# One mask instruction for two adjacency tiles, in a two-layer graph network on one core

## The reference

```python
def gat(h, W, lw, lb, a):                 # one attention layer
    Wh = h @ W
    u, v, c = Wh @ lw[:64] @ a, Wh @ lw[64:] @ a, lb @ a
    e = leaky_relu(u + v.T + c, 0.2)      # 8192 x 8192
    att = softmax(where(adj > 0, e, -9e15), axis=1)
    return elu(att @ Wh)

# layer 0
h = relu(layernorm(x)); h0 = h; outs = [h]
for i in range(2):
    h = 0.2 * h0 + 0.8 * gat(h, W[i], lin_w[i], lin_b[i], attn[i])
    outs.append(h)
x = x + concat(outs) @ mlp_w + mlp_b
# layer 1
h = relu(layernorm(x)); a = (adj == 1)
x = x + concat(a @ h / a.sum(1), h) @ weight + bias
```

## Time and profile before

| | |
|---|---|
| time, median of 3 runs | 1733.85 us (1733.81 to 1733.99) |
| the profiled execution | 1734.81 us, span 1733.0 us, granted TensorE clock 0.971 |
| TensorE busy | 1538.9 us, 89% |
| VectorE busy | 1531.3 us, 88%, 2480 instructions |
| ScalarE busy | 1289.1 us, 74% |
| the ramps (L498) | x1024, 1149 ns each |
| on masks, off masks (L919, L929) | x512 each, 691 ns each |
| conversions (L941) | x128, 2297 ns each |

### The profile page before, as it was taken

The page is one execution under the profiler, slowest core; times in us unless marked ns, Lnnn a source line. Parts: engine busy times, 40 slices in busy tenths (PEclk is TensorE's granted clock), DMA queues, the critical chain, the costliest instruction groups (busy, mean ns, idle before and its releaser), DMA issues. The chain is left out here.

```text
span 1733.0 us, 50280 instructions
## 1 busy us (share of the span) xinstructions
PE 1538.9 (89%) x21783; PEld 1495.0 (86%) x21783; DVE 1531.3 (88%) x2480; ACT 1289.1 (74%) x1470; POOL 82.2 (5%) x118
## 2 busy tenths in 40 slices
PE   2477888888888888888799999999999999799999
PEld 2377888788888888787699999999999999799999
DVE  7899999999999999999798787869688788986665
ACT  3777898989899998989699999999999994000000
POOL 1100000101010000101100000000000000000000
PEclk9589999999999999999899999999999999999999
DMA  7988999999999999997211212122121111133231
GB/s 272 356 310 311 385 378 401 356 410 376 411 372 407 387 375 407 363 410 275 61 45 44 56 45 63 42 59 62 39 63 50 57 51 32 57 116 89 86 94 44
DMA packets 114701, 356.02 MB, mean 205 GB/s; under 512 B 8976, under 2 KB 17200, under 8 KB 114480
## 3 DMA queue, kind: packets, MB, share of 16 engines
q1 hardware_dynamic: 91040, 304.27, 46.2%
q0 software_dynamic: 8960, 29.43, 6.2%
q10 hardware_dynamic: 14480, 19.11, 3.1%
HBM read 325.45 MB, written 27.33 MB: 204 GB/s over the span
## 5 line engine op out<-in xcount | busy, mean ns | idle before, releaser
L498 ACT ACTIVATE region<-ub,bigv 128x1024 uint8<-128x1024 f32 x1024 | 1096.0, 1149 | 28.6 <-PE bank L1644 11.3
L1638 PE MATMUL bank<-wsplit,region 128*128 128x195 bf16 x8192 | 788.5, 250 | 41.3 <-DVE region L919 35.4
L1638 PEld LDWEIGHTS bank<-wsplit,region 128*128 128x128 fp8e3 x8192 | 695.2, 99 | 52.8 <-DVE region L919 35.3
L1644 PE MATMUL bank<-wsplit,region 128*128 128x130 f16 x8192 | 557.7, 221 | 52.2 <-DVE region L929 50.8
L1644 PEld LDWEIGHTS bank<-wsplit,region 128*128 128x128 fp8e3 x8192 | 500.5, 98 | 77.3 <-DVE region L929 72.5
L929 DVE SCALAR_TENSOR_TENSOR region<-region 128x512 uint32<-128x512 uint32 x512 | 343.5, 691 | 9.4 <-PE bank L1644 8.6
L919 DVE SCALAR_TENSOR_TENSOR region<-region 128x512 uint32<-128x512 uint32 x512 | 338.0, 691 | 10.1 <-ACT region L498 9.9
L941 DVE TENSOR_SCALAR region<-region 128x4096 uint8<-128x4096 int32 x128 | 294.1, 2297 | 0.9 <-DMA region<-in_adj 0.9
L1865 PE MATMUL bank<-wsplit,region 128*128 128x129 f16 x4032 | 239.6, 222 | 8.8 <-DVE region L1447 8.8
L1865 PEld LDWEIGHTS bank<-wsplit,region 128*128 128x128 fp8e3 x4032 | 237.5, 99 | 10.0 <-DVE region L1447 10.0
L1447 DVE TENSOR_SCALAR region<-region 128x512 uint32<-128x512 uint32 x256 | 100.4, 424 | 43.6 <-PE bank L1865 38.4
(11 more groups left out here) (223 smaller groups left out, 686.2 us busy)
## 6 DMA issues: line engine op xcount, KB each, us to landing
region<-in_adj SPq DMA_DIRECT2D x128, 2048.0 KB, 11.3
region<-codes_d SPq DMA_DIRECT2D x128, 256.0 KB, 2.6
codes_d<-region ACTq DMA_DIRECT2D x64, 256.0 KB, 6.5
ub<-u_d POOLq DMA_DIRECT2D x16, 512.0 KB, 7.5
hg<-h_d POOLq DMA_DIRECT2D x16, 256.0 KB, 6.3
stg<-m_d POOLq DMA_DIRECT2D x16, 256.0 KB, 4.8
region<-in_x SPq DMA_DIRECT2D x4, 512.0 KB, 6.9
h_d<-wsplit POOLq DMA_DIRECT2D x4, 512.0 KB, 4.2
```

The source lines that it names most:

```text
L498: last = nc.scalar.activation(sv[:, b, :], ub[G % 2][:, :], ACT.Relu, bias=bigv[l][:, t:t + 1], scale=BIG)
L1638: return nc.tensor.matmul(acc_on[it], columns(onb[U % NS], it, b), wsplit[:, c * TC + 2 * q + b, 0:WC], start=(c == 0 and q == 0 and b == ...
L1644: return nc.tensor.matmul(acc_off[it], columns(offb[U % NO], it, b), woff[:, c * TC + 2 * q + b, WO:WO + WF], start=(c == 0 and q == 0 and ...
```

## The change

A unit becomes one quarter of two neighbouring tiles (n even and n + 1), 4 KB per partition or 1024 words: U = LU * l + 2 * n + s, with q = 2 * (n % 2) + s. The first tile step of a pair handles quarters 0 and 1 of both tiles, the second quarters 2 and 3. So VectorE issues one on mask and one off mask of 1024 words where there were two of 512. The ring of ramps has four buffers of 4 KB, the off ring three; the bytes are the same. The mean pass keeps its buffers of 2 KB (`onm`, eight of them over the same bytes). Because a unit needs the codes of both tiles, codes and weight splits run one tile further ahead, and a codes buffer is free again only when the whole pair is masked (`pair_done`). The work of ScalarE and TensorE is the same in number and size of instructions, but its order changes: all on products of a unit (32) come before all its off products. In TensorE's wait before the small products the count rises from n + 3 to n + 4.

```diff
-LU = QC * NT
+LU = 2 * NT
-NA, NP, NS, NO = 3, 4, 8, 6
+NA, NP, NS, NO, NM = 3, 4, 4, 3, 8
...
+        def pair_done(M):
+            return 2 * (M - M % 2 + 2)
...
                 def take_codes(n):
                     act.wait_ge(tp_done, n + 1)
                     if n >= NP:
-                        act.wait_ge(off_r, 4 * (n - NP) + 4)
+                        act.wait_ge(off_r, pair_done(n - NP))
...
+                take_codes(1)
+                store_codes(1)
                 for n in range(NT):                    # ScalarE, pass 0
                     g, r = n // NCH, n % NCH
-                    ramps(0, n, 0)
-                    if g == 0 and r > 0:
-                        cast_high(0, r)
-                    ramps(0, n, 1)
-                    if n + 1 < NT:
-                        take_codes(n + 1)
+                    ramps(0, n, 0, 0)
+                    if 0 < n < NCH - 1:
+                        cast_high(0, n + 1)
+                    ramps(0, n, 0, 1)
+                    if 0 < n < NT - 2:
+                        take_codes(n + 2)
                     if r == 5 and g > 0:
                         high(NG + g - 1)
-                    ramps(0, n, 2)
-                    if n + 1 < NT:
-                        store_codes(n + 1)
-                    if g == 0 and r > 0:
-                        cast_middle(0, r)
-                    ramps(0, n, 3)
+                    ramps(0, n, 1, 0)
+                    if 0 < n < NT - 2:
+                        store_codes(n + 2)
+                    if 0 < n < NCH - 1:
+                        cast_middle(0, n + 1)
+                    ramps(0, n, 1, 1)
+                    if n == 0:
+                        take_codes(2)
+                        store_codes(2)
...
                 for n in range(1, NT):                 # ScalarE, pass 1
-                    for q in range(QC):
-                        ramps(1, n, q)
-                        if g == 0 and r > 1 and q == 0:
-                            cast_high(1, r)
-                        if g == 0 and r > 1 and q == 2:
-                            cast_middle(1, r)
+                    ramps(1, n, 0, 0)
+                    if n < NCH - 1:
+                        cast_high(1, n + 1)
+                    ramps(1, n, 0, 1)
+                    ramps(1, n, 1, 0)
+                    if n < NCH - 1:
+                        cast_middle(1, n + 1)
+                    ramps(1, n, 1, 1)
...
                 split_first(0)                         # VectorE, before pass 0
+                dve.wait_ge(p_in, 2)
+                on_mask(0, 0, 0)
+                off_mask(0, 0, 0)
                 split(0, 0)
+                split(0, 1)
                 row_args(0)
                 convert(2, 1)
                 pack_pairs(2)
                 pack(2)
+                on_mask(0, 0, 1)
+                off_mask(0, 0, 1)
+                convert(3, 0)
+                convert(3, 1)
+                pack_pairs(3)
+                pack(3)
                 for n in range(NT):                    # VectorE, pass 0
-                    ahead = n + 3 < NT
-                    dve.wait_ge(p_in, n + 1)
-                    if n + 1 < NCH:
-                        split_scaled(0, n + 1)
-                    on_mask(0, n, 0)
-                    on_mask(0, n, 1)
-                    off_mask(0, n, 0)
-                    if n + 1 < NCH:
-                        split_rest(0, n + 1)
+                    ahead = n + 4 < NT
+                    if n > 0 and n % 2 == 0:
+                        dve.wait_ge(p_in, n + 2)
+                    if n + 2 < NCH:
+                        split_scaled(0, n + 2)
+                    if n > 0:
+                        on_mask(0, n, 0)
+                    if n + 2 < NCH:
+                        split_rest(0, n + 2)
                     if ahead:
-                        convert(n + 3, 0)
-                    off_mask(0, n, 1)
+                        convert(n + 4, 0)
+                    if n > 0:
+                        off_mask(0, n, 0)
...
-                    on_mask(0, n, 2)
                     if ahead:
-                        convert(n + 3, 1)
+                        convert(n + 4, 1)
...
-                    off_mask(0, n, 2)
-                    on_mask(0, n, 3)
+                    if n > 0:
+                        on_mask(0, n, 1)
                     if ahead:
-                        pack_pairs(n + 3)
+                        pack_pairs(n + 4)
-                    off_mask(0, n, 3)
+                    if n > 0:
+                        off_mask(0, n, 1)
                     if ahead:
-                        pack(n + 3)
-                    if n + 1 < NCH:
-                        split_last(0, n + 1)
+                        pack(n + 4)
+                    if n + 2 < NCH:
+                        split_last(0, n + 2)
...
                 for n in range(NT):                    # TensorE, pass 0
-                    if n + 2 < NT:
-                        transpose_codes(n + 2)
+                    if n == 1:
+                        transpose_codes(3)
+                    if 0 < n < NT - 3:
+                        transpose_codes(n + 3)
                     unit(0, n, 0)
-                    unit(0, n, 1)
+                    if n == 0:
+                        transpose_codes(2)
                     if n == 1 or (g > 0 and r >= 5) or (g > 1 and r == 0):
-                        pe.wait_ge(p_in, min(n + 3, NT))
+                        pe.wait_ge(p_in, min(n + 4, NT))
                         claim_b7()
```

More of the change, by code:

```diff
@@ L294, in _ @@
                     M = NT + n
-                    sp.wait_ge(off_r, 4 * (M - NP) + 4)
+                    sp.wait_ge(off_r, pair_done(M - NP))
                     if n == 0:
@@ L849, in split_first, with ends, four @@
                 def split_first(l):
-                    on, off = expv[:, 0:2, 0:1].to_broadcast([P, 2, CE]), expv[:, 0:2, 1:2].to_broadcast([P, 2, CE])
-                    part = [wsplit[:, 0:2, j * CE:(j + 1) * CE] for j in range(3)]
-                    hi, lo = woff[:, 0:2, WO:WO + CE], woff[:, 0:2, WO + CE:WO + WF]
-                    full, rest, small = av[:, 0:2, :], bb[:, 0:2, :], po[:, 0:2, :]
+                    def ends(ap):
+                        return ap.rearrange("p (c k) e -> p c k e", c=2)[:, :, 0:2, :]
+                    def four(buf):
+                        return buf[:, 0:4, :].rearrange("p (c k) e -> p c k e", c=2)
+                    both = slice(0, 2 * TC)
+                    on, off = [ends(expv[:, both, i:i + 1]).to_broadcast([P, 2, 2, CE]) for i in range(2)]
+                    part = [ends(wsplit[:, both, j * CE:(j + 1) * CE]) for j in range(3)]
+                    hi, lo = ends(woff[:, both, WO:WO + CE]), ends(woff[:, both, WO + CE:WO + WF])
+                    full, rest, small = four(av), four(bb), four(po)
                     dve.wait_ge(scl, l + 1)
@@ L863, in split_first @@
                     ec.sync()
-                    sc.mark(nc.vector.tensor_tensor(full, hw[:, 0:2, :], on, ALU.mult))
-                    sc.mark(nc.vector.tensor_tensor(small, hw[:, 0:2, :], off, ALU.mult))
+                    sc.mark(nc.vector.tensor_tensor(full, ends(hw[:, both, :]), on, ALU.mult))
+                    sc.mark(nc.vector.tensor_tensor(small, ends(hw[:, both, :]), off, ALU.mult))
                     sc.sync()
@@ L1211, in _ @@
                 split(1, 0)
+                split(1, 1)
                 def old_x(e):
@@ L1329, in _ @@
                     g, r = n // NCH, n % NCH
+                    if n > 0 and n % 2 == 0:
+                        codes_in(n)
+                        codes_in(n + 1)
+                    if n + 2 < NCH:
+                        split_scaled(1, n + 2)
                     if n > 0:
-                        codes_in(n)
-                        if n + 1 < NCH:
-                            split_scaled(1, n + 1)
                         on_mask(1, n, 0)
-                        on_mask(1, n, 1)
                         off_mask(1, n, 0)
-                        off_mask(1, n, 1)
-                        if n + 1 < NCH:
-                            split_rest(1, n + 1)
+                    if n + 2 < NCH:
+                        split_rest(1, n + 2)
                     if n == 1:
@@ L1389, in _ @@
                     if n > 0:
[L1390 to L1393 removed]
+                        off_mask(1, n, 1)
+                    if n + 2 < NCH:
+                        split_last(1, n + 2)
                     if n == 1:
                         row_args(1)
[L1396 to L1397 removed]
                     if g > 0:
@@ L1674, in unit @@
                             banks_free(G, it, True)
-                        for b in range(2):
-                            last = on_matmul(l, n, q, it, b)
-                            if first and G > 0 and it == 0 and b == 0:
-                                last.then_inc(off_done, 2)
+                        for h in range(2):
```

(5 more changed lines are left out.)

178 lines of the change are left out of this document (88 added, 90 removed).

## The result

The changed kernel takes 1783.89 us (median of four runs, 1782.58 to 1784.58), the kernel before 1733.83 (1733.47 to 1733.99) beside it: a ratio of 1.0289, 95% interval 1.0277 to 1.0302. That is +50 us where +39.5 was forecast, inside the range of 1750 to 1790 and on the forecast's side. The profiled execution took 1782.58 us, its span 1780.8; what follows splits 47.8 us, from a span of 1733.0 to this one.

The account below looks back on a forecast made before the run. VectorE was taken to bound pass 0 and TensorE pass 1. The terms, -18.0 + 8.6 + 14.3 + 23.2 + 1.8 + 9.6 = +39.5 us, gave 1773 us, range 1750 to 1790.

Parts of the forecast that it names:

- Step 1: VectorE's masks in pass 0: joining 512-word masks into 1024 saves 0.30 us per tile over some 60 tiles, -18.0 us.
- Step 2: Prologue: codes one tile further ahead add conversion and weight-split time before the loop, not given back, +8.6 us.
- Step 3: Weight splits of group 0: ScalarE's codes copy waits for the last off mask, delaying casts VectorE needs, +14.3 us.
- Step 4: Each later row group: the same wait makes VectorE stall 3.4 us for ramps in seven groups, +23.2 us.
- Step 5: End of pass 0: ScalarE sets the stretch from VectorE's last mask to the last group's sums, +1.8 us.
- Step 6: Start of pass 1: casts and splits delay masks, TensorE idles 6 us, then runs at lower clock, +9.6 us.
- rival (d): Adjacency loads bind in pass 0: about 1743 us without stalls, at most a few us added with them; chance 0.06.
- Rival (a): ScalarE's lead is not needed, so slack hides the stalls in pass 0 and most later delays: 1724 us; chance 0.06.
- (b): The stall at each row group's end alone is absent because the sums fall elsewhere: 1750 us; chance 0.12.
- (c): TensorE's waits for codes reach VectorE through the off buffers, about 2.5 us more in seven groups: 1790; chance 0.12.
- (e): Neighbouring 1024-word masks overlap less than starts say; a joined pair saves 0.17 us, not 0.075: 1750; chance 0.02.

Follow-up runs that it names:

- halves: The changed kernel with each mask issued as two instructions of 512 words, same place and semaphore count: 1792.40 us, ratio 1.0333 to the kernel before.
- before_ahead: The kernel before with only the codes running one tile further ahead, masks still of 512 words: 1737.69 us, ratio 1.0024 to the kernel before.
- codes_late_g0: The changed kernel with ScalarE's codes copy moved behind the ramps at even tiles of the first row group only: 1771.28 us, ratio 1.0215.
- light_loads: The changed kernel with adjacency loads behind the first three bringing only half of each half row block (output not the reference's): 1775.75 us, ratio 1.0238.
- codes_late: The changed kernel with ScalarE's codes copy moved behind all its ramps at even tiles of pass 0: 1756.37 us, ratio 1.0126 to the kernel before.
- combo: codes_late plus, at pass 1's start, tile 1's ramps ahead of ScalarE's casts and its masks ahead of VectorE's remaining splits: 1752.16 us, ratio 1.0101.
- combo_bal: combo with each tile's second conversion moved behind its second on mask: 1751.63 us, ratio 1.0102 to the kernel before.
- late_halves: codes_late with each mask issued as two instructions of 512 words: 1763.15 us, ratio 1.0167 to the kernel before.

## Where the prediction was right and where wrong, by its steps

**Step 1** had the mechanism and nearly the size. 0.30 per tile was 0.28, VectorE's work in the 52 tiles fell by 12.7 us for 15.6, and the two trials with halves give 14.9 and 19.1 us by the medians, 17.9 and 17.8 by the spans, for the 18.0. By the estimate from the initialisation that the Trainium skill lists ("VectorE: DVE Perf Modes", "Side-by-side: where the cycles go for N=2048 bf16") it would have been 39; the trace does not agree, as the starts in the earlier trace rows had shown.

**Step 2**, 8.6 us, fits what is left of the first row of the table: 21.7, less 15.6 of waits, plus 2.2 of shorter masks, is 8.3. Its terms for the splits were not measured one by one. Its sentence that nothing is given back did not hold for the lead alone: before_ahead measured +4.0 with 5.8 at tile 8. How much of that return the changed kernel keeps was not measured.

**Step 3**, 14.3 us: the waits are 15.6, 3.1 us each at split_last as worked out, and the order of the codes copy makes 11 to 12 of them (codes_late_g0). 4.0 us at split_rest stay in that order too.

**Step 4**, 3.4 us in seven groups: 3.37 or 3.38 at five, 2.74 at the first, and 1.98 at 517.75, where VectorE had just lost 1.30 in a wait for a load (509.47) and so came later to the ramps (light_loads, which has no such wait, lost 3.36 at that place); 21.6 in all for 23.2. codes_late took 15 us more than codes_late_g0 did.

**Step 5**, +1.8 against +1.4. **Step 6**, +9.6 against +8.5, with an idle time of 5.74 us for 6.

**The sum failed in the row of 52 tiles**, 16.7 for 7.6, and the missing term is rival (d): "with them the queues have time to catch up, so at most a few us are added" ("them" are the stalls). The loads added 7.0 us (7.9 for 0.9), and light_loads returned 8.1. The rest is masks 2.9 smaller, less 1.6 of smaller stalls, and 0.7 of another wait. The argument held a mean, "1.5 x 10.99 - 2.2 = 14.3 on average" and 13.8 afterwards, against the time from issue to landing, and this fails twice.

First, the three buffers do not have equal times. The two conversions of a tile stand 3.34 us apart and then 7.35 (302.84, 310.19 above). The buffer freed at 301.79 is wanted at 313.52, 11.7 us later; the one freed at 305.13 only at 320.9, 15.7 later. In before the short one is 12.1 (a conversion that begins at 371.05 and takes 2.29, the third behind it at 385.40). From issue to landing the loads of after take, from 200 to 800 us:

```profile
DMA to landing us min/median/max: 7.3/12.2/16.4
```

That is a little more than in the earlier trace rows. Read load by load in the trace, those with the short time land after 11.6 us by the median, those with the long one after 13.8. So the median is under the 11.7 that the short ones have, but not by much. Each of the ten waits of after stands at the tile's second conversion, the one with the short time. This is the longest:

```profile
562.48 2.29 DVE L970 TENSOR_SCALAR region<-region 128x4096 uint8<-128x4096 int32 x1 [2.17 <-DMA region<-in_adj]
```

Second, the time to landing is itself made of waiting. In after 98 of 99 loads from 200 to 800 us were issued while the one before was still under way. In such stretches the core moves 410 GB/s, in before and in after alike, and a tile's two loads most often take 10.8 us to land (read from one landing to the second after it), in before, after, halves, combo and combo_bal. A plain tile of VectorE takes 10.96 us in before and 10.68 in after, so with the shorter masks it asks a little faster than the loads come; in combo_bal it takes 10.80. Once in a row group four transfers that GpSimd issues take some of the queues' time, and the core moves less in all. The rows are windows with the columns of the earlier trace rows: the first is of before, the second of after, the third of after around four such transfers (349 to 353 us).

```profile
340.00:385.00 45.00, 39.67 (x525) 37.05 (x524) 45.00 (x51) 37.72 (x51) 0.00 (x0) 0.96 1.03 410
```

```profile
366.00:411.00 45.00, 37.94 (x500) 36.97 (x499) 43.69 (x34) 39.07 (x41) 0.00 (x0) 0.92 1.03 410
340.00:362.00 22.00, 19.42 (x276) 19.02 (x274) 21.96 (x23) 18.94 (x27) 4.47 (x4) 1.00 0.95 302
```

Eight of the ten waits come 17 to 30 us behind the first of such four. A stall of 3.4 us does give the queues time, as the prediction said: the short-time loads behind it land after 7 to 9 us. It comes once in eight tiles, and the lead is gone again at the next four transfers. Whether the uneven times or the rate of the loads cost more is open: halves and late_halves keep the order and have a tile of 10.96, and their waits for loads are 3.5 for 7.9 and 2.4 for 9.3 us; combo_bal changed the order and the length of the tile at once. No run changed the order alone.

**Rival (a)** and **(b)** are excluded by the wait lines. **(c)** is too: TensorE did wait for codes, 27.5 us and 25.8 at two lines in 215 to 900 us, but VectorE never waited for TensorE in the 52 tiles. **(e)** fell with halves.

Of the 11 us between forecast and run, 8.3 are in the sum (47.8 for 39.5). The rest is that the profiled execution of after lay 1.3 us under its median and that of before 1.0 over its own.

## What to carry to other kernels

Joining two instructions into one saves the distance from start to start, which must be read in the trace (0.28 us per tile here), and makes every hand-over twice as coarse: list each instruction of the partner engine that waits for the whole, and all that stands behind it. A single copy that waited for the last mask of a pair made all that was queued behind it late, and moving it behind the ramps returned 27.5 of 50 us; one wait too early in an engine's order can cost more than the change was to bring. For a ring of buffers, compare first the distance at which loads land when the queue is never empty (two in 10.8 us here) with the time in which they are used up (10.68): the time from issue to landing contains waiting behind other loads, and by itself it does not show how near the loads are to their limit. Where the buffers are freed at uneven distances, look at the shortest interval too, not at the mean alone.

## What was not expected of the hardware

In these rows VectorE starts an instruction later when it reads what the one right ahead of it wrote. Behind a conversion that was 2.31 us for 2.20 (combo_bal), and behind an on mask 1.32 for 1.13 (927.01 to 928.33 at the start of pass 1, where the off mask follows its on mask at once). In the program each of these instructions also waits for the semaphore of the one ahead; no run tells the reading from the waiting. In combo_bal 0.12 us a tile, 7 us in all, were enough to cancel 8.5 us of shorter waits. The adjacency loads of half the size landed 4.9 us after their issue by the median, where whole ones took 12.2, more than twice as long. Part of the 12.2 is waiting: nearly every whole load was issued while the one before was under way, and only 50 of 100 half ones.
